# Expert results added to the output in DRAM by accumulating scatters, in place of a read-back and sums at the end

## The reference, cut to what matters

```
x = x + tanh(g_xattn[0]) * xattn(ctx_2048, layernorm(x), ...)
x = x + tanh(g_ffn[0]) * ffn(layernorm(x), ...)

# ffn: 2048 tokens, 9 experts, top 2
scores = sigmoid(x_flat @ gate.T + bias)
top_scores, selected = top_k(scores, 2)
top_scores = top_scores / (sum(top_scores) + 1e-20)
for e in range(9):
    h = silu(x_flat @ ew1[e].T) * (x_flat @ ew3[e].T)     # hidden width 352
    out = out + cw[:, e:e+1] * (h @ ew2[e].T)             # cw is 0 for experts not chosen
```

## Time and profile before

| what | value |
| --- | --- |
| time, median of 3 runs | 218.54 us (217.89 to 218.61) |
| profiled execution: span | 234.1 us; the page shows no other time of this execution, and nothing of it ahead of or behind the span |
| PE busy | 205.4 us (88% of the span) |
| DVE, ACT, POOL busy | 149.6, 142.7 and 128.8 us |
| POOL, scatters of `yt` (L616) | 38, 37.8 us, 995 ns each |
| POOL, scatters into `x_rows` (L593) | 32, 32.7 us, 1022 ns each |
| mean granted TensorE clock | 0.968 |

### The profile page before, as it was taken

The page is one execution under the profiler, slowest core; times in us unless marked ns, Lnnn a source line. Parts: engine busy times, 40 slices in busy tenths (PEclk is TensorE's granted clock), DMA queues, the critical chain, the costliest instruction groups (busy, mean ns, idle before and its releaser), DMA issues.

```text
span 234.1 us, 5788 instructions
## 1 busy us (share of the span) xinstructions
PE 205.4 (88%) x1606; PEld 166.9 (71%) x1606; DVE 149.6 (64%) x523; ACT 142.7 (61%) x399; POOL 128.8 (55%) x230
## 2 busy tenths in 40 slices
PE   8999986999999999898883946299999999999981
PEld 3577653666666676565573945299999999999881
DVE  0469997788898698897865822344443444456774
ACT  2286869988778876786471620266667666666210
POOL 4237745132325876786783578556675756557320
PEclk9999999999999999999998897589999999999998
DMA  5999999999910100011372221121222221261194
GB/s 164 368 377 242 407 381 409 408 370 318 342 55 13 36 23 26 23 36 38 86 214 62 61 76 49 41 53 55 61 69 68 52 65 47 49 218 53 37 348 163
DMA packets 23602, 34.91 MB, mean 149 GB/s; under 512 B 2562, under 2 KB 15879, under 8 KB 23443
## 3 DMA queue, kind: packets, MB, share of 16 engines
q1 hardware_dynamic: 20610, 29.27, 37.9%
q0 software_dynamic: 2240, 4.23, 5.5%
q10 hardware_dynamic: 720, 1.02, 1.5%
HBM read 15.85 MB, written 19.06 MB: 149 GB/s over the span
## 4 chain that ended last, share of the span: by engine, by line
PE 56%; DVE 14%; another core or an unknown queue 7%; ACT 6%; DMA 6%; issue 5%; POOL 4%; SPq 1%; POOLq 0%; DVEq 0%; ACTq 0%
PE pt_ps L1363 10%; PE score_ps L1321 5%; PE pt_ps L1372 4%; PE score_ps L1323 4%; PE score_ps L1322 4%; PE score_ps L1176 4%; DMA kheads<-y_rows 3%; PE pt_ps L1116 3%; PE ps_a L1226 3%; PE pt_ps L1214 3%; PE score_ps L1126 2%; PE ps_b L1283 2%; DVE less L827 2%; ACT probs L401 2%
## 5 line engine op out<-in xcount | busy, mean ns | idle before, releaser
L616 POOL DMA_INDIRECT y_rows<-vals,ids x38 | 37.8, 995 | 17.2 <-ACT vals L473 9.6
L1363 PE MATMUL pt_ps<-w,probsT 128*128 x234 | 34.4, 285 | 14.6 <-ACT probsT L480 6.7
L1363 PEld LDWEIGHTS pt_ps<-w,probsT 128*128 128x128 f32 x234 | 32.1, 198 | 15.9 <-issue 15.8
L593 POOL DMA_INDIRECT x_rows<-stage,slot x32 | 32.7, 1022 | 10.4 <-issue 7.7
L401 ACT ACTIVATE probs<-score_ps,less 128x128 f32<-128x128 f32 x128 | 37.9, 419 | 0.4 <-DVE less L827 0.4
L1043 DVE TENSOR_TENSOR xg_low<-ps_a,xg_high 128x128 fp32r<-128x128 f32 x40 | 11.7, 291 | 37.1 <-issue 23.6
L473 ACT ACTIVATE vals<-pt_ps,xg 128x128 f32<-128x128 f32 x38 | 14.0, 368 | 34.4 <-PE pt_ps L1363 24.7
L1321 PE MATMUL score_ps<-w_high,xg_low 128*128 x80 | 30.3, 379 | 0.0
L1051 DVE TENSOR_TENSOR probs<-probs,score_ps 128x352 f32<-128x352 f32 x40 | 20.8, 521 | 11.2 <-PE score_ps L1323 5.3
L1323 PE MATMUL score_ps<-w_high,xg_high 128*128 x80 | 26.6, 332 | 0.0
L1322 PE MATMUL score_ps<-w_low,xg_high 128*128 x80 | 26.5, 332 | 0.0
(11 more groups left out here) (179 smaller groups left out, 445.6 us busy)
## 6 DMA issues: line engine op xcount, KB each, us to landing
x_rows<-pads SPq DMA_DIRECT2D x1, 9945.0 KB, 37.3
w_low<-in_w13T SPq DMA_DIRECT2D x3, 1056.0 KB, 11.0
xg<-x_rows SPq DMA_DIRECT2D x40, 65.0 KB
ctx_r<-in_ctxT SPq DMA_DIRECT2D x4, 512.0 KB, 7.7
y_rows<-pads SPq DMA_DIRECT2D x1, 2048.0 KB, 16.6
w<-in_w2T SPq DMA_DIRECT2D x1, 1728.0 KB, 11.2
kheads<-y_rows SPq DMA_DIRECT2D x3, 512.0 KB, 5.0
mask_b<-in_mask SPq DMA_DIRECT2D x4, 256.0 KB, 8.0
```

Source lines behind the costliest of these rows:

```text
L593: pool.indirect_dma_start(x_rows[:, :], bass.IndirectOffsetOnAxis(ap=slot[:, par, c, p:p + 1], axis=0), stage[:, par, c, p, :], None, boun ...
L616: pool.indirect_dma_start(y_rows[:, :], bass.IndirectOffsetOnAxis(ap=ids[:, s:s + 1], axis=0), yt[:, s, :], None, bounds_check=last_row, o ...
L1363: last = nc.tensor.matmul(into[:, 0:D], hidT[:, q3, c, :], w2[:, bass.ds(e3, 1), c, :].rearrange("p o d -> p (o d)"), start=(c == 0), stop ...
```

## The change

There is no `y_rows` any more. A scatter of `yt` now adds to the output rows in DRAM, which hold x2 (`compute_op=ALU.add`); a row number is simply the token's number. Two scatters that both add to one row must not overlap, and this can happen only between tiles of different experts. So there are two semaphores for the scatters, used in turn; a scatter waits for the one two tiles earlier always, and for the one just before it if its tile's expert is another, or if its tile is the first of a table (0, 8, 16) or is tile 1 or 2. Where that is not known ahead, DVE writes the count to wait for into `landed`, and POOL loads it into a register. Tile 0's scatter waits for x2 in the output. Pad rows are no longer left out: DVE caps their numbers (`cast_ids`) to one of two spare blocks of 128 rows behind the output, so that they are added there. All 40 tiles are scattered, and the kernel ends when the last two scatters have landed. The copy of the row numbers on POOL, the spare memsets, the read-backs, the sums and the final stores are gone. The core of the diff:

```diff
-SUMMED = 2
+TURNS = 2
+FIRSTS = [sum(TILES[:n]) for n in range(len(TILES))]
+        def scattered(t):
+            return t // TURNS * 16 + 16
             # SP
-            sp.dma_start(y_rows.rearrange("(p n) d -> p n d", p=P), pads[:, 0:1, 0:D].to_broadcast([P, 2 * NB, D])).then_inc(st_zero, 16)
+            sp.dma_start(out[NB * P:(NB + TURNS) * P].rearrange("(n p) d -> p n d", p=P), pads[:, 0:TURNS, 0:D]).then_inc(st_zero, 16)
...
-            sp.dma_start(xs[:], out_tok).then_inc(x2_back, 16)
-            for place in range(YR):
-                sp.wait_ge(st_y[place], len(range(place, NT - SUMMED, YR)) * 16)
-            for g, here in enumerate(PARTS):
-                sp.dma_start(ys[:, here, :, :], y_tok[:, here, :, :]).then_inc(ld_y[g], 16)
-            for g, here in enumerate(PARTS):
...
-                sp.dma_start(out_tok[:, here, :], xs[:, here, :]).then_inc(st_out, 16)
+            for n in range(TURNS):
+                sp.wait_ge(st_y[n], scattered(NT - TURNS + n))
             # ACT, before it writes a place of yt again
-                        act.wait_ge(st_y[t % YR], t // YR * 16)
+                        act.wait_ge(st_y[t % TURNS], scattered(t - YR))
             # POOL
-            def tile(k, r):
-                s = k % YR
-                pool.wait_ge(ids_cast, k + 1)
-                if k >= YR:
-                    pool.wait_ge(st_y[s], k // YR * 16)
-                nc.gpsimd.tensor_tensor(ids[:, s:s + 1], ids_in[:, s:s + 1], zero[:], ALU.add).then_inc(ids_copied, 1)
-                pool.wait_ge(ids_copied, k + 1)
+            def tile(k):
+                s, turn = k % YR, k % TURNS
+                if k in FIRSTS or k <= TURNS:
+                    if k >= 1:
+                        pool.wait_ge(st_y[(k - 1) % TURNS], scattered(k - 1))
+                else:
+                    if k - 1 in FIRSTS or k == TURNS + 1:
+                        pool.wait_ge(landed_known, sum(f < k for f in FIRSTS))
+                    pool.wait_ge(st_y[(k - 1) % TURNS], pool.value_load(landed[0:1, k:k + 1], min_val=16, max_val=16 * NT))
+                    pool.sem_inc(rows_apart, 1)
                 if k == 0:
                     pool.wait_ge(st_zero, 16)
-                if k < 3 * TR:
-                    short_space()
+                    pool.wait_ge(x2_stored, 16)
+                if k >= TURNS:
+                    pool.wait_ge(st_y[turn], scattered(k - TURNS))
+                pool.wait_ge(ids_cast, k + 1)
                 pool.wait_ge(y_done, k + 1)
-                pool.indirect_dma_start(y_rows[:, :], bass.IndirectOffsetOnAxis(ap=ids[:, s:s + 1], axis=0), yt[:, s, :], None,
-                                        bounds_check=last_row, oob_is_err=False).then_inc(st_y[s], 16)
+                pool.indirect_dma_start(out[:, :], bass.IndirectOffsetOnAxis(ap=ids[:, s:s + 1], axis=0), yt[:, s, :], None,
+                                        bounds_check=last_row, oob_is_err=True, compute_op=ALU.add).then_inc(st_y[turn], 16)
...
             # DVE, in table_rows
+                nc.vector.tensor_tensor(changed[:, 1:tiles], expert_f[:, 1:tiles], expert_f[:, 0:tiles - 1], ALU.not_equal)
...
+                nc.vector.scalar_tensor_tensor(landed[:, at + 1:at + tiles], changed[:, 1:tiles], 16.0, part["landed"][0:1, at + 1:at + tiles],
+                                               ALU.mult, ALU.add).then_inc(landed_known, 1)
             # DVE, cast_ids
                 if t >= YR:
-                    dve.wait_ge(ids_copied, t + 1 - YR)
-                nc.vector.tensor_copy(ids_in[:, t % YR:t % YR + 1], xg[:, place, C_ID:C_ID + 1]).then_inc(ids_cast, 1)
+                    dve.wait_ge(st_y[t % TURNS], scattered(t - YR))
+                nc.vector.tensor_scalar(ids[:, t % YR:t % YR + 1], xg[:, place, C_ID:C_ID + 1], part["nowhere"][:, t % TURNS:t % TURNS + 1], None,
+                                        ALU.min).then_inc(ids_cast, 1)
             # host
+        "landed": 16 * ((np.arange(NT) - 1) // TURNS),
```

More of the change, by code:

```diff
@@ L61, with build @@
 FIRST = {"ident": P, "head_rows": HH, "gates": 2, "b_key": 1, "b_qry": 1, "b_val": D}
-CONSTS = {"mask_t": NB, "b_res": D, "rows_below": P, "experts": NE, "first_rows": NE, "first_ids": 2 * UN, "nowhere": 1, "gate_b": NE, "rows_of": P, "blocks": NB}
-ROW_CONSTS = {"first_tiles": NE, "experts_upto": NE * NE, "tiles": NT, "digits": NT}
+CONSTS = {"mask_t": NB, "b_res": D, "rows_below": P, "experts": NE, "first_rows": NE, "first_ids": 2 * UN, "nowhere": TURNS, "gate_b": NE}
+ROW_CONSTS = {"first_tiles": NE, "experts_upto": NE * NE, "tiles": NT, "digits": NT, "landed": NT}
 ROUNDER = 1.5 * 2.0 ** 23
 NCTX, WARM = 3, 24
-def build(nc, x, ctxT, mask, first, consts, row_consts, w_srcT, w_tgtT, w_outT, w13T, w2T, gateT, x_rows, y_rows, out):
+def build(nc, x, ctxT, mask, first, consts, row_consts, w_srcT, w_tgtT, w_outT, w13T, w2T, gateT, x_rows, out):
     with ExitStack() as ctx:
@@ L174, in build @@
         st_last = [sem(f"st_last{n}") for n in range(UN)]
-        st_y = [sem(f"st_y{n}") for n in range(YR)]
-        ld_y = [sem(f"ld_y{n}") for n in range(len(PARTS))]
-        x2_stored, x2_back, st_out = sem("x2_stored"), sem("x2_back"), sem("st_out")
+        st_y = [sem(f"st_y{n}") for n in range(TURNS)]
+        x2_stored, landed_known, rows_apart = sem("x2_stored"), sem("landed_known"), sem("rows_apart")
         dve_chain, act_chain, pool_set, table_chain = sem("dve_chain"), sem("act_chain"), sem("pool_set"), sem("table_chain")
@@ L520, in _ @@
             pool.wait_ge(ld_rest, 16)
-            nc.gpsimd.tensor_copy(pads[:, :, C_ID], part["nowhere"].to_broadcast([P, NE])).then_inc(pad_set, 1)
+            nc.gpsimd.memset(pads[:, :, C_ID:C_ID + 1], float(NOWHERE)).then_inc(pad_set, 1)
             rstd(1)
@@ L626, in _ @@
             scatter(NG - 2, 3)
-            for k in range(NT - SUMMED):
-                tile(k, k % TR)
+            for k in range(NT):
+                tile(k)
                 if k == 1:
@@ L631, in _ @@
                         scatter(NG - 1, p)
-            pool.wait_ge(x2_back, 16)
-            here = PARTS[BY_POOL]
-            pool.wait_ge(last_out, 1)
-            nc.gpsimd.tensor_tensor(xs[:, here, :], xs[:, here, :], chosen_rows[:, 0, here, :], ALU.add).then_inc(last_added, 1)
         @block.vector
@@ L806, in weigh @@
                                                ALU.mult, ALU.mult).then_inc(weighed, 1)
-                nc.vector.tensor_scalar(stage[:, g % 2, :, :, C_ID], part["first_ids"].rearrange("p (c b) -> p c b", c=2), 2.0 * UN * P * g, None, ALU.add)
+                nc.vector.tensor_scalar(stage[:, g % 2, :, :, C_ID], part["first_ids"].rearrange("p (c b) -> p c b", c=2), float(UN * P * g), None, ALU.add)
                 assert route_links["weigh"] == LINKS["weigh"]
@@ L1054, in tile @@
                     turn = i if r >= 3 else i - 1
[L1055 to L1060 removed]
+                    cast_ids(t, place, turn)
                 if is_last(k - 1):
@@ L1472 @@
     args = [nc.dram_tensor(k, v.shape, mybir.dt.from_np(v.dtype), kind="ExternalInput").ap() for k, v in arrays.items()]
-    out = nc.dram_tensor("out_0", (NB, P, D), F32, kind="ExternalOutput").ap()
+    out = nc.dram_tensor("out_0", ((NB + TURNS) * P, D), F32, kind="ExternalOutput").ap()
     x_rows = nc.dram_tensor("x_rows", (NE * CAP + P, RW), F32).ap()
-    y_rows = nc.dram_tensor("y_rows", (2 * NB * P, D), F32).ap()
-    build(nc, *args, x_rows, y_rows, out)
+    build(nc, *args, x_rows, out)
     r = run_bass_kernel_spmd(nc, [arrays], core_ids=[0])
-    return r.results[0]["out_0"]
+    return r.results[0]["out_0"][:NB * P].reshape(NB, P, D)
```

125 lines of the change are left out of this document (10 added, 115 removed).

## The result

The changed kernel takes 272.13 us (median of 4 runs, 270.74 to 272.95), the kernel before 218.21 us in the same comparison (4 runs): a ratio of 1.247, with a 95% interval of 1.241 to 1.253. It is slower, as forecast, but by 54 us and not by 22; 240 us was predicted, with a range of 220 to 266. The profiled execution of the changed kernel took 272.42 us, of which its span is 270.5.

A forecast was written before the change was run, and what follows sets the result against it. PE bounds the old tiles; the change makes a chain of POOL scatters set the end. Start 139.9 us plus 100.3 (23 waiting steps of 3.19, 14 others of 1.74, a landing of 2.5) gives 240.2, forecast 240, range 220 to 266.

The forecast's parts named there:

- wake-up: On POOL, from a landing's semaphore to the start of the next scatter: 0.69 us, as several waits stand ahead.
- standstills: Four pauses of ACT in the tile stage of the profiled execution, 15.79 us together; absent from the shown runs with chance 0.6.
- x2's store: Start of POOL's chain: the store, issued at 118.27 us, would not delay tile 0's scatter at 128.41; 0.8 us to spare.
- P: POOL's price of a step that waits for the scatter before it: landing 2.5 plus wake-up 0.69, 3.19 us.
- the issue itself takes much more than 1 us: Sign of a wrong forecast, on POOL's scatters: P would be right or wrong for a reason not priced.
- The rival of a dear read: Adding scatters on POOL: landing 4.04 us, P 4.73, 277 us or more; chance 0.20 for 255 to 281.
- G: POOL's price of a step that does not wait: issue 0.99, register load and arithmetic, 0.31 between scatters; 1.74 us.
- the gain of 11.0 us for the removed end: Behind the last result: 14.2 us go, one wake-up and one landing stay, if POOL kept up; end at 223.1.
- the places just suffice: ACT and DVE writing the 16 places again: at P = 3.19 PE shows little of the wait for POOL.
- POOL keeping up: Rival, POOL's scatter chain: P 2.41 with standstills in the timed runs, 210 us; chance of faster 0.12.
- The case in which the waits do not bind: Rival case, POOL's scatters: the waits cost nothing, end at 223.1, so 207.5 us; no chance of its own given.
- The cheap wait of the rivals: Rival, POOL's wake-up where one wait stands ahead: 0.28 us; without standstills P 2.58, 226 us; chance 0.13.

The follow-up runs named there:

- experiment 1: The kernel before, unchanged, profiled once more: 218.63 us with a span of 216.8.
- experiment 2: The changed kernel with all its waits, but its scatters overwrite rows in place of adding: 242.37 us, ratio 1.112 to the kernel before.
- experiment 4: The changed kernel with plain scatters into a row for each result, no waits between scatters, no read-back or final sums: 214.18 us, ratio 0.981.
- experiment 3: The changed kernel with adding scatters into a row for each result, no waits between scatters, no read-back or final sums: 219.06 us, ratio 1.003.
- experiment 5: The changed kernel with the experts' order written in as constants, so POOL loads no register for its waits: 260.29 us, ratio 1.199.
- 5 to 7: Besides 5: 6 is 5 with the landing's wait written last, 272.2 us; 7 is 5 with a counting instruction behind the landing's wait, 274.19 us.
- 9: The kernel before, with POOL's one closing addition given to PE as a product with the identity: 217.38 us, ratio 0.998.

## Why the prediction was right in direction and wrong in size

**What was right.** The chain of waits runs along POOL and its scatters from 142 us to the end. In the view of that chain it does so from 175 us on; ahead of that the view follows PE, but the steps of 4.2 us, a landing and a wake-up each, begin at 142.13. PE is done 43 us before the last scatter (219.6 against 262.80). The order of the experts and so the counts of steps came out: 14 steps do not wait. The standstills were not in the timed runs (experiment 1), as taken with a chance of 0.6. What the removed end gives is less than what the chain costs, x2's store did not hold up tile 0, and the new table work on DVE ends at 138 us, ahead of tile 2.

**The step that failed: the price P of a waiting step.** It was 2.5 + 0.69 = 3.19 us and is 4.17 on average. Its parts:

| part of P | forecast | measured | by |
| --- | --- | --- | --- |
| issue on POOL | 0.99 | 1.54 | +0.55 |
| rest of the landing | 1.51 | 1.76 | +0.25 |
| wake-up | 0.69 | 0.87 | +0.18 |

The forecast took the issue over from the earlier trace rows and the landing from plain scatters, "the same instruction with the same bytes", and put the whole doubt about adding into the flight. Half of the price of adding, 0.57 us of some 1.1 a step (experiment 2), is on POOL itself. The wake-up was read from a row in which POOL waits ahead of the scatter; that its price hangs on this place was not seen. The text named "the issue itself takes much more than 1 us" as something that it had not priced; that case occurred, and the range had no room for it beside the other terms. The rival of a dear read had the landing at 4.04 us and named 277 us or more. In total it lies nearer to the result than the forecast, but its price, 1.74 us more for a read entirely ahead of the write, is not what is seen: the flight grew by some 0.5 us from experiment 2 to the changed kernel (2.2 - 0.97 = 1.2, against 3.3 - 1.54 = 1.8). The Trainium skill's 2 us for an HBM access under load (page "DMA: Bandwidth & Descriptors", section "Latency and other measured facts") gave an estimate of 4.3 for the landing in the prediction, its 0.2 us one of 2.5; the 3.3 measured lies between, and the longer issue is in neither.

The sum with measured terms, against 240.2:

| term | us |
| --- | --- |
| 21 waiting steps of 4.17 and two of 3.58 (tiles 8 and 16), not 23 of 3.19 | +21.4 |
| 14 steps of 1.85, not 1.74 | +1.5 |
| tile 2 starts at 142.13, not 139.9 | +2.2 |
| last landing 3.3, not 2.5 | +0.8 |
| from the last landing to the end of the span (POOL's DRAIN) | +4.4 |
| a run's time outside its span | +1.9 |
| sum | +32.2 |

240.2 + 32.2 = 272.4, against 272.42 measured for the profiled run. Two thirds of the miss is P.

**The other terms.** G was nearly right for wrong reasons: the register load (0.42) is hidden beside the issue, the issue is 0.55 longer, and the two errors nearly cancel. The start: experiment 1 has the last of the eight `x_rows` scatters through, with its 0.30, at 140.3, so the shift by one standstill was right to 0.4 us. In the changed kernel the slots come later than there (131.02 against 129.78), and tile 1, held until tile 0 has landed (129.97 above), keeps POOL for about 0.5 us more. The forecast had let tile 1 pass ahead of the slots with 0.8 us to spare; the dearer landing and issue used that up. The DRAIN was not in the forecast at all: the old kernel's span ends hardly later than SP, so it did not stand out there. And the span was set equal to the time, since the first page had no other time; experiment 1 shows 1.8 us between them. For the same reason the gain of 11.0 us for the removed end was too high, whatever P is: 14.2 us lie behind the last result in experiment 1 too (202.63 to 216.8), but where nothing waits (experiment 4) 8.6 us are left (203.73 to 212.3), not the 3.2 of one wake-up and one landing, and the kernel gains 3.95 us.

**The places.** That "the places just suffice" was wrong as well, as a consequence of P: ACT and DVE wait 27.7 and 22.0 us for them. It costs nothing further, since they wait for the chain that sets the end.

**The rivals.** POOL keeping up (210) could not have happened: by experiment 3 the issue alone, 1.85 us a tile from 140.5, ends at 209.0, and the kernel takes 219. The case in which the waits do not bind (207.5) is nearest to experiment 4, at 214.18 even without the addition. There SP is done at 207.6, as priced, and DRAIN and the time outside the span make up the difference. The cheap wait of the rivals, 0.28 us, does exist: it is the 0.29 of experiment 5, but with the landing of an adding scatter the kernel then takes 260 us and not 226.

## What to carry to other kernels

An instruction with one option more is not the instruction in the trace: before a sum over 40 of them, bound its issue on the engine and not only its flight, and give the range room for both. A chain that waits for landings costs issue, flight and wake-up at each link; two targets in turn took it down to the issue (220 us against 260), while cheaper waits alone did not. Where an engine waits for several semaphores, let the one that comes last stand on the working instruction itself, which here meant writing it first: for POOL's scatters that was 0.6 us a step, 12 us in all, for one line's place.

## What the runs showed of the hardware

- A scatter of 128 rows of 512 bytes that adds takes 1.54 us to issue on POOL and lands after 3.3 us; the plain one takes 0.97 and 2.2 (the changed kernel and experiments 2 to 4). The adding one is 144 DMA packets, the plain one 32.
- With the wait that comes last on the scatter itself, it starts 0.29 us after the landing; with that wait on an event instruction ahead, 0.75 to 0.9 us (5 to 7, and the changed kernel).
- POOL's closing DRAIN ends 5.8 to 6.0 us after POOL's last instruction: 270.3 against 264.34 in the changed kernel, 216.6 against 210.78 in experiment 1, 212.06 against 206.09 in experiment 4. It does so whether that instruction was a scatter or an addition. A kernel whose last work is on POOL pays for it.
- A sum on DVE of 128 x 512 took 1.76 us beside an addition on POOL, 0.69 us without (1 and 9).
